# A three-layer graph network on one core: in the second convolution ScalarE writes the bias ahead of the squares, and VectorE takes the variance of x2 after the aggregations

## The reference

```python
def gcn_conv(x, W, b, src, dst, n_nodes):
    xw = x @ W
    # self-loops appended to src and dst; norm = deg^-1/2[s] * deg^-1/2[d]
    msg = norm[:, None] * xw[s]
    return jax.ops.segment_sum(msg, d, num_segments=n_nodes) + b

h = relu(layernorm(x))
residual = h
h = gelu(layer_norm(gcn_conv(h, W1, b1), gamma1, beta1))            # convolution 1
h = layer_norm(gcn_conv(h, W2, b2), gamma2, beta2)                  # convolution 2
x = x + gelu(h + residual)                                          # this is x2
h = relu(layernorm(x))
x = x + gcn_conv(h, W, b)                                           # convolution 3
```

## Time and profile before

| | before |
|---|---|
| median of 3 runs | 3242.31 us (3240.88 to 3243.55) |
| the profiled execution | 3241.1 us |
| its span in the trace | 3239.2 us |
| busy PE / PEld / DVE | 2906.8 / 2431.8 / 2557.8 us |
| busy ACT / POOL | 2050.9 / 2071.3 us |

### The profile page before, as it was taken

The page is one execution under the profiler, slowest core; times in us unless marked ns, Lnnn a source line. Parts: engine busy times, 40 slices in busy tenths (PEclk is TensorE's granted clock), DMA queues, the critical chain, the costliest instruction groups (busy, mean ns, idle before and its releaser), DMA issues. The chain is left out here.

```text
span 3239.2 us, 60605 instructions
## 1 busy us (share of the span) xinstructions
PE 2906.8 (90%) x16427; PEld 2431.8 (75%) x16427; DVE 2557.8 (79%) x6373; ACT 2050.9 (63%) x3083; POOL 2071.3 (64%) x1615
## 2 busy tenths in 40 slices
PE   8223359999999999799999999999879999999999
PEld 2122258888888888688888888888768888888888
DVE  9899968888888888699999999999934444544444
ACT  0256557777776777599999999999833333333333
POOL 0122257777777776588888888888655555555553
PEclk9999999999999999899999999999989999999999
DMA  3399988888888886699999999999789999999996
GB/s 134 150 372 418 416 245 214 213 217 220 214 216 216 216 217 174 217 328 331 330 328 330 330 327 325 331 328 329 271 239 286 288 288 291 286 287 287 287 289 206
DMA packets 304977, 890.18 MB, mean 275 GB/s; under 512 B 67209, under 2 KB 67707, under 8 KB 304922
## 3 DMA queue, kind: packets, MB, share of 16 engines
q1 hardware_dynamic: 189082, 681.53, 60.6%
q0 software_dynamic: 115840, 208.01, 27.0%
HBM read 652.74 MB, written 307.71 MB: 297 GB/s over the span
## 5 line engine op out<-in xcount | busy, mean ns | idle before, releaser
L842 POOL DMA_INDIRECT gathered<-H,idx x826 | 1155.2, 1399 | 515.7 <-issue 245.5
L1230 PE MATMUL out<-Whi,ahi 128*128 128x512 f32 x2832 | 778.6, 397 | 10.0 <-ACT out L925 3.0
L916 ACT ACTIVATE ahi<-agg 128x1024 fp32r<-128x1024 f32 x354 | 360.9, 1019 | 642.6 <-PE agg L1221 642.6
L1230 PE MATMUL out<-Wlo,ahi 128*128 128x512 f32 x2832 | 760.0, 390 | 0.0
L1230 PE MATMUL out<-Whi,alo 128*128 128x512 f32 x2832 | 739.2, 390 | 0.1
L1230 PEld LDWEIGHTS out<-Wlo,ahi 128*128 128x128 f32 x2832 | 532.5, 188 | 115.7
L1230 PEld LDWEIGHTS out<-Whi,alo 128*128 128x128 f32 x2832 | 531.5, 188 | 110.9 <-DVE alo L1041 0.5
L1230 PEld LDWEIGHTS out<-Whi,ahi 128*128 128x128 f32 x2832 | 509.3, 189 | 119.3 <-ACT out L925 26.8
L1033 DVE TENSOR_TENSOR vlo<-gathered,vhi 128x512 fp32r<-128x512 f32 x354 | 242.7, 686 | 317.4 <-ACT vhi L910 317.4
L925 ACT ACTIVATE out<-vec,sqrt_deg 128x512 f32<-128x512 f32 x708 | 457.9, 681 | 14.7 <-PEq L750 8.1
L1041 DVE TENSOR_TENSOR alo<-agg,ahi 128x1024 fp32r<-128x1024 f32 x354 | 428.4, 1210 | 24.6 <-ACT ahi L916 24.4
(11 more groups left out here) (162 smaller groups left out, 3755.0 us busy)
## 6 DMA issues: line engine op xcount, KB each, us to landing
gathered<-H SPq DMA_DIRECT2D x351, 512.0 KB, 6.2
H<-ho SPq DMA_DIRECT2D x250, 512.0 KB, 4.5
x<-in_x_dram SPq DMA_DIRECT2D x165, 512.0 KB, 7.0
X<-x SPq DMA_DIRECT2D x117, 512.0 KB, 8.9
x<-X SPq DMA_DIRECT2D x117, 512.0 KB, 7.5
out_dram<-conv SPq DMA_DIRECT2D x117, 512.0 KB, 9.3
H<-x SPq DMA_DIRECT2D x48, 512.0 KB, 9.6
gathered<-H,idx POOLq DMA_INDIRECT x826, 5.7
```

The source lines that it names most:

```text
L842: pool.indirect_dma_start(rows, None, H[q][0:end, :], bass.IndirectOffsetOnAxis(ap=idx[p.slot(4)][:, c:c + 1], axis=0), bounds_check=end - ...
L916: nc.scalar.activation(Ahi[p.slot(2)][:, :], Agg[p.slot(2)][:, :], ACT.Copy)\
L1230: m = nc.tensor.matmul(Out[2 * p.slot(2) + j][:, :], a[p.slot(2)][:, c:c + P], w[q][:, f, :], start=False, stop=stop and f == KD - 1, skip ...
```

## The change

Three edits, all in convolution 2. On ScalarE `seed` of pair p+2 stands ahead of `squares` of p-1, and no longer between `gelu` and `relu_x2`. On VectorE `x2_var_eps` of p-2 stands between `mean_var` and `var_eps` of p, and no longer ahead of `mean_var`. And `normal` waits for `rstd_done` only where `x2_scale`, which waits for the same value in the same turn, isn't there.

```diff
                         if second:
+                            if has(known, 2):
+                                seed(of(known, 2), p.after(2))
                             if has(known, -1):
                                 squares(p.after(-1))
                             if has(known, 2):
                                 high(p.after(2))
                             if has(known, 0):
                                 gelu(p)
-                            if has(known, 2):
-                                seed(of(known, 2), p.after(2))
                             if has(known, -2):
                                 relu_x2(of(known, -2), p.after(-2))
...
                         if j == 0:
-                            dve.wait_ge(rstd_done.sem, rstd_done.upto(p))
+                            if first or not has(known, -2):
+                                dve.wait_ge(rstd_done.sem, rstd_done.upto(p))
                             dve.wait_ge(cg_done.sem, cg_done.upto(p))
...
-                        if second and has(known, -2):
-                            v = x2_var_eps(p.after(-2))
-                            if not has(known, 0):
-                                v.then_inc(ve_done.sem, 1)
                         if third:
                             if has(known, 0):
                                 result(known, p)
                             return
                         if has(known, 0):
                             mean_var(p)
+                        if second and has(known, -2):
+                            v = x2_var_eps(p.after(-2))
+                            if not has(known, 0):
+                                v.then_inc(ve_done.sem, 1)
+                        if has(known, 0):
                             var_eps(p)
                             centre(p)
```

## The result

The changed kernel takes 3223.27 us (median of 4 runs, 3221.35 to 3223.7) against 3242.51 for the kernel before (4 runs, one more than in the table above; 3240.88 to 3243.55): a ratio of 0.994, 95% interval 0.9923 to 0.9957, 19 us faster. The forecast was 3222.2. The profiled execution took 3222.98 us, 18.1 less than that of before, with a span of 3221.1 us.

A forecast was written before the change was run, and what follows sets the result against it. The prediction took a ring through VectorE and GpSimd's additions, 8.53 us a pair, as the bound. 106 x 0.19 = 20.1 us off the profiled 3241.1 gives 3221.0, plus 1.2 for the median: 3222.2 us, range 3214 to 3243.

The forecast's parts named there:

- The hold: VectorE's `x2_var_eps` stands still until GpSimd's additions of `residual` end; moving it saves 0.19 us a pair.
- The variance hides in the wait behind the aggregations: On VectorE, the moved variance fits into the 0.37 us before `var_eps`, costing nothing; `var_eps` itself isn't held.
- The wait taken out: Between `x2_scale` and `normal` on VectorE: could give 0 to 0.10 us; taken as 0, ScalarE's path being as long.
- the ring: Chain closing in one period: `residual`, held variance to `var_eps`, next mean, `sv`, `residual` again; together 8.53 us.
- The sum: Whole kernel: 106 held instructions x 0.19 = 20.1 us saved, giving 3222.2 us, 0.62% less.
- The seed, put at 0: Seed ahead of `squares` on ScalarE: TensorE's 0.25 us wait disappears, but TensorE isn't in the limiting chain, so worth 0.
- slack of 0.38: ScalarE's idle time in front of `squares`, 0.57 us before the change, becomes 0.57 - 0.19 = 0.38.
- a sign that I had named as being wrong: On ScalarE, a wait for `seed` or for a DMA appearing would show the prediction wrong; DMA waits were costed at 0.
- The variance in its own slot: On VectorE the variance takes 0.10 us at its new place; gain only 9.5 us, 3232.8 us; chance 0.13.
- More than forecast: Variance gain and some of the removed wait both count until TensorE's 8.32 us limits: 26.5 us, 3215.8; chance 0.07.
- No change: An unseen chain, GpSimd the candidate, is equally long and keeps the period at 8.57 us: 3242.3 us; chance 0.11.
- A gather held for longer: GpSimd's second gather lasts 1.90 us, not 1.46, when `vlo` follows sooner; `residual` starts late: 3255 us; chance 0.14.

The follow-up runs named there:

- e5: The kernel before with GpSimd's two additions of `residual` over 256 of the 512 columns, nothing moved on VectorE: 3222.99 us, 0.9946 of before.
- e1: The kernel before with only the variance of x2 moved behind the aggregations: 3224.65 us, 0.9955 of before.
- e6: The kernel before with the variance of x2 as a single-input `tensor_scalar`, epsilon a constant, in the same place: 3239.64 us, 1.0001 of before.
- e9: The kernel before with the variance as a single-input `tensor_scalar` over three columns in place of two: 3240.16 us, 0.9998 of before.
- e11: e8 with the 128x3 copy of `indices` moved into VectorE's wait between statistics and aggregation: 3229.68 us, 0.9966 of before.
- e12: e8 with GpSimd's `gather_over` made to wait for `var_eps` of the same turn: 3318.13 us, 1.0237 of before.
- e8: The changed kernel with `high` of pair p+2 put ahead of `squares` on ScalarE: 3215.43 us, 0.9927 of before.
- e3: The kernel before with only the repeated wait of `normal` taken out: 3233.21 us, 0.998 of before.
- e2: The kernel before with only the seed moved ahead of the squares on ScalarE: 3240.65 us, 1.0004 of before.
- e4: The changed kernel with the repeated wait put back, so only variance and seed are moved: 3225.63 us, 0.9959 of before.
- e7: The whole change measured again with no edit, on the chip of other follow-up kernels: 3220.98 us, 0.9942 of before.
- e10: The kernel before with only `high` of pair p+2 put ahead of `squares` on ScalarE: 3238.24 us, 0.9995 of before.

## Why the prediction was right, and where it wasn't

**The hold, and what bounds the kernel.** Right, and shown from both sides: shortening the additions (e5) and moving the variance (e1) each free it, and other instructions put in its place are held instead (e6, e9, e11). The saving at `stats` to aggregation was sized at 0.19 and measured 0.182 to 0.184. (That VectorE has no wait in the list was not quite so: it has three, 0.7 us in all.)

**The variance hides in the wait behind the aggregations.** Right for the variance itself: it lasts 131 ns, and aggregation to `var_eps` grew by 0.013 just as in e5, where it doesn't stand there. What the step missed is `var_eps`: I checked it against the end of the additions, 0.12 ahead of it, and not against the gather that GpSimd starts 0.15 behind that end. With the variance gone `var_eps` arrives at just that start and is held by up to 0.07. The variance alone was thus worth 0.132 a turn and 15 us, not 20.1. That the gather is what holds it is shown by e1, where the hold shrinks with the distance to the gather's start, and by e12, where the gather is out of the way, the additions are as near as in e8, and the hold is gone.

**The wait taken out, put at 0.** Wrong. Alone it was worth 6 us. The kernel before has the ring from the mean to `sv` and from there to the additions, never through `low`, and in e3 I priced the edit at `low` all the same; in that ring nearly the full 0.07 counts. With the variance moved, the ring does go through `low`, as the prediction has it, and there ScalarE's path did limit the gain, to 0.035 at the most (e3) where I allowed 0.03. The edit still gives 8.438 - 8.404 = 0.034 there: 0.017 at `low`, less 0.008 between `low` and `stats`, and 0.030 at `var_eps`. `sv` comes 0.07 earlier and the gather with it, while `var_eps` comes hardly earlier, so that the two part and the hold shrinks. The prediction has no term for this.

**The sum.** 20.1 + 0 was forecast and 19 came, as 15 from the variance and 4 to 6 from the wait. Two errors of some 5 us met with opposite signs. That the total came within about 1 us of the forecast is luck; the terms were not that good.

**The seed, put at 0.** Right to the accuracy of the runs, alone (e2) and beside the variance (e4). ScalarE's slack of 0.38 was 0.44. But a sign that I had named as being wrong did come: ScalarE waits for a DMA, for the gathered rows of `over_high` and not for the load of x that I had looked at. Such waits are there in the runs with the seed moved (e2, e4, the whole change and e7, e8, and e11 on top of e8), and in none of before, e1, e3 and e10. In the whole change, where `low` hangs on `high`, they cost about 1.7 us, and in e7 about 1.0 (three late turns). Without the six turns the period of the changed kernel is 8.388, close to the 8.38 of the forecast. The other two edits without the seed were not run, so it is not shown that they would be faster by that much.

**Rivals.** *The variance in its own slot*: no. *More than forecast*: there was room, but ScalarE's squares and not TensorE stood in it first; e8 took 5.5 us of it and ended at a period of 8.368, 0.05 above what I gave TensorE. *No change*: no chain as long as the ring was hidden. *A gather held for longer*: the gathers became 0.03 shorter on average (1.396 for 1.423 us), so they do move up with VectorE as I argued. The distance from the second one to `vlo` fell from 0.58 to 0.51 at the median, but in none of the 108 turns did it lie between 0.22 and 0.43, and the longest gather took 1.54 us. Nothing went that way. In e8 one turn did: distance 0.35, gather 1.90.

## What to carry to other kernels

An engine that never waits in the list can still be waiting inside an instruction: look for a tiny operation whose duration is several times that of its like, and for what ends on another engine when it ends. Write the ring down edge by edge, and price every edit by whether its stretch is an edge of that ring, not by what else is as long as the stretch; with several edits, write down the ring that the others leave, too. And when an instruction is freed, check the ones that now arrive earlier against everything that the other engine starts next, not only against what held the first.

## What the runs showed of the hardware that I had not expected

A small VectorE instruction on SBUF alone that started beside a GpSimd addition was held to the end of the additions whether it had two inputs (489 ns), one input over two columns (496 ns), one input over three (497 ns), or was a 128x3 copy (502 ns); free, such an instruction takes 131 to 163 ns. The aggregation, which also reads and writes SBUF alone, isn't held: in the turn of the changed kernel shown above two of them run from 1820.57 to 1820.82, the additions until 1820.80, and they last 0.25 us, as long as where GpSimd adds nothing. Over all turns one lasts 168 ns at the median in e1, beside the additions, and 166 in e5, where the additions are over before it. The Trainium skill (SBUF — State Buffer, Who interferes with whom) explains the two-input forms by the shared read port and the others by a mode that uses both ports; the rows agree with both, but none tells the two apart.

The start of an indirect DMA on GpSimd held a small VectorE instruction with two inputs, but only for a moment: `var_eps` ended some 0.19 us behind the start of the DMA's row where it came within 0.03 us of it (e1, e8), and was not held where it came 0.15 or more behind (before), though the DMA's row lasts 1.03 us.

A wait of an indirect DMA on GpSimd for VectorE, where the wait wasn't already satisfied, cost about 1 us from the end of the VectorE instruction to the start of the DMA's row (e12), five times what the elementwise `residual` takes behind `sv` (0.18 to 0.19). What the time goes into no run shows.
